# A three-stage graph-network kernel, first stage: masks of the last quads in two banks, preparation of the next unit from its first step, measured step weights in the planner, blocks spaced otherwise

## What is computed

```python
def _adapt_conv(h, edge_weight, W, b, is_last):
    h = h @ W + b
    norm = jnp.linalg.norm(h, axis=-1, keepdims=True)
    nh = h / jnp.maximum(norm, EPS)
    cos = jnp.einsum('bij,bkj->bik', nh, nh)
    ew = edge_weight * cos
    h = jnp.einsum('bpq,bqc->bpc', ew, h)
```

```python
def step(carry, n):
    row = jnp.take(carry, n, axis=0)
    nbi = row.astype(jnp.int32)
    num = jnp.sum(nbi)
    sf = jnp.where(num > T_DIL, (num + K_DIL - 1) // K_DIL, 1)
    rank = jnp.cumsum(nbi)
    rm = row & (rank % sf == 0)
    ...
    carry = carry.at[n].set(row & keep)
    carry = carry.at[:, n].set(carry[:, n] & keep)
```

## Time and profile before

| | us |
|---|---|
| median of three runs | 2920.18 |
| lowest | 2915.8 |
| profiled execution | 2917.8 |
| its span, first to last instruction | 2915.9 |

### The profile page before, as it was taken

The page is one execution under the profiler, slowest core; times in us unless marked ns, Lnnn a source line. Parts: engine busy times, 40 slices in busy tenths (PEclk is TensorE's granted clock), DMA queues, the critical chain, the costliest instruction groups (busy, mean ns, idle before and its releaser), DMA issues. The chain is left out here.

```text
span 2915.9 us, 41242 instructions
## 1 busy us (share of the span) xinstructions
PE 2709.7 (93%) x13446; PEld 1717.0 (59%) x13446; DVE 2193.0 (75%) x5582; ACT 1280.8 (44%) x3780; POOL 1088.6 (37%) x493
## 2 busy tenths in 40 slices
PE   6999999899999999999999994999999969999997
PEld 4666566566556566666665652555555545554886
DVE  5788899899888889899998864666656525675567
ACT  2555554554534554455545300232333224443665
POOL 4333424233044342432400003766666603442661
PEclk9999999899999999999999996999999979999998
DMA  7364364274174473373351014355555318996653
GB/s 237 101 216 135 105 211 138 71 234 147 35 230 138 129 239 105 103 249 114 110 184 50 21 56 155 118 208 208 210 194 188 116 72 327 396 397 243 231 204 129
DMA packets 322509, 492.29 MB, mean 169 GB/s; under 512 B 20592, under 2 KB 214512, under 8 KB 322288
## 3 DMA queue, kind: packets, MB, share of 16 engines
q1 hardware_dynamic: 322288, 489.57, 48.7%
HBM read 422.38 MB, written 67.11 MB: 168 GB/s over the span
## 5 line engine op out<-in xcount | busy, mean ns | idle before, releaser
L582 POOL TENSOR_SCALAR a_T<-a_ats 128x512 uint8<-128x512 f32 x256 | 510.6, 2004 | 936.4 <-DMA a_ats<-in_adjT 935.2
L657 PE MATMUL a_acc<-a_ew,a_Hr 128*128 128x512 f32 x1536 | 769.3, 606 | 0.0
L830 DVE TENSOR_TENSOR a_ew<-adj,a_cos 128x512 f32<-128x512 f32 x768 | 512.4, 682 | 108.4 <-PE a_cos L650 106.9
L648 PE MATMUL a_cos<-a_nh 128*128 128x512 f32 x768 | 423.3, 551 | 26.0 <-DVE a_nl L822 25.5
L657 PEld LDWEIGHTS a_acc<-a_ew,a_Hr 128*128 128x128 f32 x1536 | 272.6, 192 | 134.5 <-issue 95.6
L769 ACT ACTIVATE a_v<-a_D,a_wb,a_small 128x256 f16<-128x256 f32 x512 | 260.8, 561 | 171.4 <-PE a_D L693 170.6
L1425 POOL TENSOR_TENSOR b_dsum<-adj 128x1024 f32<-128x1024 f32 x16 | 142.2, 8886 | 488.3 <-DVE adj L1379 488.3
L650 PE MATMUL a_cos<-a_nh,a_nl 128*128 128x512 f32 x768 | 308.5, 402 | 0.0
L649 PE MATMUL a_cos<-a_nl,a_nh 128*128 128x512 f32 x768 | 305.8, 398 | 0.0
L759 ACT ACTIVATE a_vr<-a_D,a_small 128x128 f16<-128x128 f32 x560 | 210.3, 458 | 185.3 <-DVE a_small L894 185.0
L1269 PE MATMUL b_acc<-adj,b_h 128*128 128x512 f32 x512 | 225.2, 598 | 21.7 <-DVE adj L1379 21.7
(11 more groups left out here) (205 smaller groups left out, 4444.2 us busy)
## 6 DMA issues: line engine op xcount, KB each, us to landing
adj<-in_adjT SPq DMA_DIRECT2D x108, 1024.0 KB, 12.5
adj<-in_adjT SPq DMA_DIRECT2D x128, 512.0 KB, 4.3
a_ats<-in_adjT SPq DMA_DIRECT2D x256, 256.0 KB, 3.3
a_af<-in_adj SPq DMA_DIRECT2D x256, 256.0 KB, 3.9
scr_keep<-a_kp SPq DMA_DIRECT2D x256, 64.0 KB, 1.6
b_kp<-scr_keep SPq DMA_DIRECT2D x16, 1024.0 KB, 7.5
c_zi<-scr_z SPq DMA_DIRECT2D x32, 512.0 KB, 5.8
c_ai<-scr_ag SPq DMA_DIRECT2D x32, 512.0 KB, 6.8
```

Source lines behind the costliest of these rows:

```text
L582: e.tensor_scalar(TT[:, Q * (quad % 2) + i, 4 * h:4 * h + 4, blk(k)].bitcast(U8), ats[h][:], 0.0, ONE8, ALU.is_gt, ALU.mult).then_inc(T["a ...
L648: e.matmul(cos[j][:], n[:, blk(k)], n[:, half(j)], start=True, stop=False)
L657: e.matmul(acc[j][:], Hr[u % 2][:, k, :], ew[idx % EW][:], start=(k == 0), stop=(k == NK - 1)).then_inc(E["agg"], 1)
L830: e.tensor_tensor(ew[idx % EW][:], adj[g % 2][:, k, half(j)], cos[j][:], ALU.mult).then_inc(E["ew"], 1)
```

## The change

Constants and the planner's input change, and the last quads' masks may use D0. No instruction is added or taken away, and no wait in the units is changed. With lines left out:

```diff
-PACE = 18.6
+PACE = 22
 AHEAD = 26
+MID = 1
+SQ = 1
...
-TAIL = {"pe": 60, "act": 150, "dve": 90, "pool": 150, "sp": 0, "dma": 2000}
+TAIL = {"pe": 60, "act": 130, "dve": 90, "pool": 150, "sp": 0, "dma": 2000}
...
+def bank_of(quad, i, q, j):
+    return "D0" if quad > 1 and j and q % 2 else "D1"
...
-        soon, mid = ([("pe", "agg", 16 * (v - 1) + n)] if v else [] for n in (1, 4))
+        soon, mid = ([("pe", "agg", 16 * (v - 1) + n)] if v else [] for n in (0, MID))
...
-            add("act", ("sq", v, c), 970, 3, [("dve", "hb", v)], "sq")
+            add("act", ("sq", v, c), 585, SQ, [("dve", "hb", v)], "sq")
...
-        add("pe", ("cos", idx), 740, 3, ([("dve", "ho", u)] if idx % 16 == 0 else []) +
+        add("pe", ("cos", idx), 700 if PAIRS and idx % 2 else 776, 3, ([("dve", "ho", u)] if idx % 16 == 0 else []) +
...
-            add("act", ("rank", n, r), 1830, 1, [("dve", "rule", n, r)], None, None, "D0")
+            add("act", ("rank", n, r), 1365, 1, [("dve", "rule", n, r)], None, None, "D0")
...
-                add("act", ("wide", n, i, j), 1140, 1, [("pe", "wide", n, i, j), ("dve", "bias", n)], None, "v", "D1")
+                add("act", ("wide", n, i, j), 900, 1, [("pe", "wide", n, i, j), ("dve", "bias", n)], None, "v", "D1")
...
-                        add("dve", ("mask", quad, i, q, j), 600, 3, [("pe", "mask", quad, i, q, j)], None, "kp", "D1")
+                        add("dve", ("mask", quad, i, q, j), 600, 3, [("pe", "mask", quad, i, q, j)], None, "kp",
+                            bank_of(quad, i, q, j))
...
-            def second_bank_free():
-                if user:
-                    kind, *a = user[-1]
+            def take(bank, step):
+                if users[bank]:
+                    kind, *a = users[bank][-1]
                     if kind == "base":
                         e.wait_ge(T["b0"], nth["dve", "base", a[0]])
+                    elif kind == "rank":
+                        e.wait_ge(T["vr"], Q * nth["act", "rank", a[0], a[1]])
```

More of the change, by code:

```diff
@@ L331, in prepare @@
             add("pe", ("lnc", g), 880, 0, [("dve", "lnb", g)] + bank)
-            add("act", ("lnc", g), 1030, 0, [("pe", "lnc", g)] + ([("pe", "posta", v - 2)] if g > 1 else []))
+            add("act", ("lnc", g), 920, 0, [("pe", "lnc", g)] + ([("pe", "posta", v - 2)] if g > 1 else []))
             bank[:] = [("act", "lnc", g)]
@@ L341, in prepare @@
         add("pe", ("hf", v), 880, 0, [("dve", "hd", v)])
-        add("act", ("hf", v), 1030, 1, [("pe", "hf", v)] + ([("pe", "cos", 16 * (v - 2) + 15)] if v > 1 else []))
+        add("act", ("hf", v), 920, 1, [("pe", "hf", v)] + ([("pe", "cos", 16 * (v - 2) + 15)] if v > 1 else []))
         add("dve", ("ho", v), 1134, 1, [("act", "hf", v)])
@@ L361, in agg @@
         if idx % 16 >= 14:
-            add("act", ("evac", u, j), 605, 0, [("pe", "agg", idx)] +
+            add("act", ("evac", u, j), 490, 0, [("pe", "agg", idx)] +
                 ([("pe", "posta", u - 1)] if u and UNITS[u - 1][1] == 2 else []), "evac")
@@ L411, in plan_dilation @@
                          None, "af")
-                add("act", ("row", n, i, j), 635, 2, [("dma", "row", n, i, j)], None, None, "af")
+                add("act", ("row", n, i, j), 520, 2, [("dma", "row", n, i, j)], None, None, "af")
         filled = [("pool", "fill", quad, k, i, h) for i in range(Q) for h in range(2)]
@@ L440, in plan_dilation @@
                             [("dve", "wide", quad * NK + b, i, c) for b, c in
-                             [(b, q // 4) for b in range(4 * j, 4 * j + 4)] + [(q, j)]], None, "D1")
-                        add("dve", ("mask", quad, i, q, j), 600, 3, [("pe", "mask", quad, i, q, j)], None, "kp", "D1")
+                             [(b, q // 4) for b in range(4 * j, 4 * j + 4)] + [(q, j)]], None, bank_of(quad, i, q, j))
+                        add("dve", ("mask", quad, i, q, j), 600, 3, [("pe", "mask", quad, i, q, j)], None, "kp",
+                            bank_of(quad, i, q, j))
                         transfer(("mask", quad, i, q, j), 250, [("dve", "mask", quad, i, q, j)], None, None, "kp")
@@ L491, in layer0 @@
         D0, D1 = P.ps("D0", [128, Q, 128]), P.ps("D1", [128, Q, 128])
+        D = {"D0": D0, "D1": D1}
         mv4 = C["mv"][:].rearrange("p (g k) -> p g k", k=NK)
@@ L605, in second_bank_free @@
                         e.wait_ge(T["kp"], nth["dve", "mask", a[0], a[1], a[2], a[3]])
-            user = []
+                users[bank].append(step)
+            users = {"D0": [], "D1": []}
             for step in plan["pe"]:
@@ L662, in pe @@
                     block_ready(n)
-                    second_bank_free()
+                    take("D1", step)
                     others = [q for q in range(NK) if q != k]
@@ L671, in pe @@
                     t.then_inc(T["bs"], 1)
-                    user.append(step)
                 elif kind == "rank":
                     n, r = a
-                    p, c = n // NK % 2, nth["pe", "rank", n, r] - 1
+                    p = n // NK % 2
                     if r:
@@ L679, in pe @@
                         block_ready(n)
-                    if c:
-                        e.wait_ge(T["vr"], Q * nth[("act", "rank") + of["pe", "rank"][c - 1]])
+                    take("D0", step)
                     for i in range(Q):
@@ L703, in pe @@
                                            + [nth["dve", "wide", quad * NK + q, i, j]]))
-                    second_bank_free()
+                    bank = bank_of(quad, i, q, j)
+                    take(bank, step)
                     for b in range(4):
-                        t = e.matmul(D1[:, b, :], slab[:, q, blk(4 * j + b)], C["ident8"][:], start=True, stop=True)
+                        t = e.matmul(D[bank][:, b, :], slab[:, q, blk(4 * j + b)], C["ident8"][:], start=True, stop=True)
                     t.then_inc(T["tr"], 1)
-                    user.append(step)
         def act(e):
@@ L942, in dve @@
                     e.wait_ge(T["tr"], nth["pe", "mask", quad, i, q, j])
[L943 removed]
+                    e.scalar_tensor_tensor(kp[c % 3][:].rearrange("p (q c) -> p q c", c=128),
+                                           D[bank_of(quad, i, q, j)][:], 0.5,
                                            TT[:, Q * (quad % 2) + i, 4 * j:4 * j + 4, blk(q)],
```

## The result

| | us |
|---|---|
| before, median of 4 runs | 2919.3 |
| after, median of 4 runs | 2811.8 (2806.2 to 2815.4) |
| ratio | 0.9634, 95% interval 0.9611 to 0.9657 |
| after, span of the profiled execution | 2811.9 (before 2915.9) |

The forecast was 2836 us with a range of 2800 to 2885. The direction held and the time lies in the range; the change brought 107.5 us where 84 were forecast. One of the four runs of the kernel before took 4306.7 us; the median counts it, and the ratio leaves it out.

A forecast was written before the change was run, and what follows sets the result against it. TensorE bounds the first stage, losing time to waits, a lowered clock and masks behind the last `agg`. Terms -20.8 - 39 - 24 = -83.8 from 2917.8 us gave 2834, 2836 with the median's 0.1%; range 2800 to 2885.

The forecast's parts named there:

- end of the stage, net: Behind the last `agg`: no masks remain, freeing 25.0 us, with 4.2 us of mask transposes put back; net -20.8 us.
- idle time of TensorE before the last `agg`: First stage from 60 us: TensorE's waits fall from 76 to 37 us, -39 us.
- clock: First stage: taking clusters of waits apart wins back 24 of 33 us lost to TensorE's lower clock; bounds 0 and -42.
- the other signs of being right: No mask behind last `agg`; next part within 7 us; `nl` under 3 us, `kp` under 8; clock 0.99 or above.
- `nl`: TensorE's wait before a unit's first `cos`, 23.2 us, goes almost whole through preparing the next unit earlier: -22 us.
- `kp` before masks: TensorE's 19.4 us wait for VectorE to empty D1 shrinks by spacing masks and wides and using D0: -15 us.
- `v`: TensorE's 13.3 us wait before a `wide` for ScalarE to empty D1 shrinks little: -5 us, within 0 to -13.
- have no price of their own: Measured ScalarE weights in the planner and closer block spacing get no separate term; they act through the priced waits.
- What comes back: First stage: VectorE at 92% density still leaves TensorE 37 us idle, so idle time falls 39 us rather than 42.
- VectorE holds the pace: Rival: the tail goes, but VectorE at 92% makes TensorE's waits only change names; 2870 to 2899 us, chance 0.18.
- `hf` as the stand: Rival: the `ha` to `hf` chain, about 9 us, makes `hf` late; 0.5 us each or more 0.08, any slowdown 0.04.
- The rival that the second bank and the spacing do nothing: Mask waits stay, so the sum lacks 15 us and half the clock term, 12: 2863 us, chance 0.08.

The follow-up runs named there:

- one version: The changed kernel with the planner's cost for ScalarE's wide step set to 1000 ns instead of 900; 2804.3 us, ratio 0.9611.

## Why the prediction was right, point by point

The mechanism held in its three terms, the end, the waits and the clock. The part of the change to which the waits were put down did not hold. Two of the three terms came out larger than forecast and none smaller, so no error hid another. The stage shrank by 103.5 us. By the terms of the sum:

| term | forecast | measured |
|---|---|---|
| end of the stage, net | -20.8 | -21.2 (-25.4 measured, 4.2 put back as reckoned) |
| idle time of TensorE before the last `agg` | -39 | -47.6 |
| clock | -24 | -34.7 (the remainder) |
| sum | -83.8 | -103.5 |

**The end.** Right in mechanism and size: from the end of the last `agg` to the next part 31.6 us before (1737.4 to 1769.0) and 6.2 after, 25.4 freed where 25.0 were reckoned. The 4.2 us put back are the forecast's own and were not measured apart. The first stage ended 103.5 us earlier, more than the 80 to 90 us given as a sign of being right; the other signs of being right came as said.

**The waits by name.** `nl` -22.8 (forecast -22) and `kp` before masks -15.2 (-15) came as said; `v` was to give 5 and gave nothing (+1.5). But the part of the change to which each was put down was wrong. `nl` does not need the earlier preparation: without it the row is 4.6 us, and the weights alone bring it to 7.7. The mask waits do not need the second bank: with it alone they are 20.4 us, with the weights alone 4.7, with the spacing alone 5.6. The term of 15 us named the masks in D0 as part of its cause, and they could give little: they stand in the last units, and only 3.2 of the 19.4 us lie behind 1400 us in the trace before. The sentence that the weights "have no price of their own" is the worst of the text: alone they bring 60 us, the largest share of any part. What the preparation and the weights have in common is that either takes nearly all of it from the middle: waits of about 30 us, clock 1.00. They do not add, so undoing one shows next to nothing there.

**What comes back.** This term was mis-sized, and so the forecast was 9 us short in idle time: I expected VectorE's density of 92% to leave TensorE 37 us idle, by today's stretches of like density. Measured are 92% and 28.8 us, and one version has 17.3. A stretch at 96% beside a TensorE at 99.9% shows that density by itself leaves no idle time; in the old trace it went together with an order made from wrong costs. With that the rival "VectorE holds the pace" fell, and its mark, 40 us of waits for `ew`, `low` or `Sd`, is absent (`ew` 0.2).

**The clock.** Mechanism right, size short by 11 us. I took 24 of 33 us back; everything came back, since no window of 10 us from 60 us to the last `agg` shows a clock below 0.97. The 34.7 us are what the other terms leave, not a measurement. As a check: by the table of the orders 41 us of clock were not granted before, and 31 us when each window counts only by the share in which TensorE was busy, so some 3 us of the 34.7 may be something else. The pair of kernels with added pauses shows why so much can hang on 48 us of idle time: the same pauses cost 25 us more when clustered.

**The other rivals.** `hf` as the stand: the row for `tmp` is 4.0 us in 6 waits, against 7.8 in 9. The chain from `ha` to `hf`, estimated at about 9 us, has a median of 9.6. It is 9.7 with the preparation undone, and 9.8 with the weights alone, but 11.8 with the weights undone: the weights shortened it, not the rank of the squares. The rival that the second bank and the spacing do nothing is wrong for the kernel: undoing the one lengthened it by 32 us, the other by 17. Its reasoning looked only at waits and not at what the planner does with a bank.

**What the text did not look at** is that the end and the middle are bought separately: weights or preparation for the middle; for the end the second bank, the weights and the spacing, each of which undone leaves 27 to 36 masks behind the last `agg`. These counts come from the planner's order alone and could have stood in the forecast.

## What to carry to other kernels

When an order is made from a table of step costs, correct the costs from the trace first: costs of ScalarE that were 12 to 66% above the new ones, with a cost of `cos` and a `TAIL` beside them, cost this kernel 60 us, more than any other single part brought. Price a reordering by its order at the end of the stage as well as by the waits of its middle: the earlier preparation alone gained 98 us in the one and lost 85 in the other. Undo parts one by one and also add them one by one; parts that each suffice look worthless when only undone.

## What was not expected of the hardware

The same pauses of TensorE, 282 products in 47 places or 286 in 11, cost 62.8 and 88.9 us, and the mean clock was 1.00 and 0.97. Waits of 28.8 us in 1595, the longest 2.5 us, left the clock of the changed kernel at 1.00 throughout. Waits of 76 us in 1675, partly in clusters, went with some 30 to 35 us of lost clock in the kernel before, though none of them was longer than 2.6 us. A product of six columns that is waited for before the next one goes lengthened the kernel by 0.22 us each (62.8 us for 282); in the trace a row of six takes 1.39 us.
